# Attention: q loaded straight into the block-diagonal operand, instead of copied there by VectorE

## The reference, cut to what matters

```python
x = x + 0.5 * ffn(layernorm(x))          # weights and activations rounded to FP6 in blocks of 32
x = x + attention(layernorm(x))
x = x + 0.5 * ffn(layernorm(x))

# attention: 16 heads of 32, each token sees 13 neighbours (K = 13, NS = 6)
q, k, v = split(x @ qkv_w.T + qkv_b); q = q * 32 ** -0.5
ni = clip(i - NS, 0, L - K)              # first neighbour of token i
attn = softmax(einsum('bhld,bhlkd->bhlk', q, k[ni + j]) + rpb[:, bidx])
out = einsum('bhlk,bhlkd->bhld', attn, v[ni + j]) @ proj_w.T + proj_b
```

## Time and profile before

| | |
|---|---|
| runs | 3541.88, 3539.46, 3540.44 us |
| span of the profiled execution, first to last instruction | 3541.7 us |
| first phase with the setup | 0 to 1743 us |
| attention | 1743 to 3029 us |
| last phase | 3029 to 3541.7 us |
| busy share of the span: TensorE, VectorE, ScalarE, GpSimd | 82%, 78%, 57%, 56% |
| mean granted TensorE clock | 0.931 |

### The profile page before, as it was taken

One profiled execution on the slowest core, in us unless ns is written; L12 is line 12 of the kernel. 1 busy time (PEld: TensorE's weight loads), 2 busy tenths in 40 slices (PEclk: granted clock), 3 DMA queues, 4 the chain that ended last, 5 costly groups with the idle time before them and its releaser, 6 DMA issues. The chain is left out here.

```text
span 3541.7 us, 67789 instructions
## 1 busy us (share of the span) xinstructions
PE 2897.5 (82%) x24864; PEld 1690.4 (48%) x24864; DVE 2759.5 (78%) x3553; ACT 2021.9 (57%) x2451; POOL 1993.0 (56%) x1497
## 2 busy tenths in 40 slices
PE   0399999999999999999677777777777777399999
PEld 0244444444444444444356555555555555244444
DVE  7366666666666666666599999999999998599995
ACT  3355556555556555564566666666666657466553
POOL 3454455544555445543166665666666666588883
PEclk9699999999999999999889988999999889699999
DMA  2123332333323332332465554555555553234432
GB/s 72 60 84 119 108 108 95 108 111 115 102 101 107 107 119 93 103 114 84 146 175 163 170 170 148 166 161 179 152 162 162 169 160 98 107 143 155 153 142 83
DMA packets 274586, 449.41 MB, mean 127 GB/s; under 512 B 15368, under 2 KB 181280, under 8 KB 266144
## 3 DMA queue, kind: packets, MB, share of 16 engines
q1 hardware_dynamic: 274336, 445.54, 39.4%
HBM read 243.85 MB, written 201.38 MB: 126 GB/s over the span
## 5 line engine op out<-in xcount | busy, mean ns | idle before, releaser
L761 DVE TENSOR_TENSOR fq_out_lo<-fq_val,fq_out_hi 128x512 f16<-128x512 f32 x384 | 460.6, 1237 | 289.8 <-ACT fq_out_hi L825 289.8
L1125 DVE COPY att_q_bd<-att_q_in 32x1024 f16<-32x1024 f16 x512 | 624.0, 1219 | 5.9 <-DMA att_q_in<-q_parts 0.7
L942 PE MATMUL fq_acc<-fq_y_hi_t,w_qkv 128*128 128x512 f16 x2048 | 614.3, 379 | 1.6 <-ACT fq_y_hi_t L838 1.6
L825 ACT CAST fq_out_hi<-fq_val 128x512 f16<-128x512 f32 x384 | 237.2, 618 | 318.9 <-DVE fq_val L758 310.8
L1250 PE MATMUL att_s_ps<-att_k,att_q_bd 128*128 128x44 f16 x6144 | 192.0, 187 | 271.2 <-DVE att_q_bd L1125 251.0
L942 PE MATMUL fq_acc<-fq_y_lo_t,w_qkv 128*128 128x512 f16 x1024 | 388.1, 379 | 0.0
L1228 POOL TENSOR_TENSOR att_score<-att_score,att_rtotal 128x704 f32<-128x704 f32 x128 | 211.2, 1650 | 226.3 <-DVE att_rtotal L1116 226.3
L1210 POOL TENSOR_TENSOR att_score<-att_score,att_top 128x704 f32<-128x704 f32 x128 | 188.3, 1471 | 245.1 <-DVE att_top L1105 245.1
L1165 ACT ACTIVATE att_ctx<-att_o_ps 32x512 f32<-32x512 f32 x512 | 300.6, 587 | 44.8 <-PE att_o_ps L1275 38.6
L1285 PE MATMUL att_y_ps<-w_proj,att_ctx_t_hi 128*128 128x512 f16 x1024 | 320.3, 396 | 2.4 <-DVE att_x L1150 2.2
L1250 PEld LDWEIGHTS att_s_ps<-att_k,att_q_bd 128*128 128x128 f16 x6144 | 178.8, 100 | 290.9 <-issue 238.3
(11 more groups left out here) (189 smaller groups left out, 6707.1 us busy)
## 6 DMA issues: line engine op xcount, KB each, us to landing
att_v<-v_parts SPq DMA_DIRECT2D x96, 704.0 KB
att_k<-k_parts SPq DMA_DIRECT2D x64, 524.0 KB, 7.4
fq_x<-in_L_attn_x SPq DMA_DIRECT2D x32, 1024.0 KB, 6.9
x_after_ffn<-fq_x SPq DMA_DIRECT2D x32, 1024.0 KB, 4.3
att_q_in<-q_parts SPq DMA_DIRECT2D x32, 1024.0 KB, 7.2
att_x<-x_after_ffn SPq DMA_DIRECT2D x32, 1024.0 KB, 5.6
x_after_attention<-att_x SPq DMA_DIRECT2D x32, 1024.0 KB, 4.3
ffn_x_ring<-x_after_attention SPq DMA_DIRECT2D x32, 1024.0 KB, 6.2
```

Source lines behind the costliest of these rows:

```text
L761: dve.tensor_tensor(out=out[1][:, b], in0=val[:, b % RING], in1=out[0][:, b], op=ALU.subtract).then_inc(s["out_lo"], 1)
L825: act.copy(out[0][:, b], val[:, b % RING]).then_inc(s["out_hi"], 1)
L942: op = pe.matmul(acc[:, b % RING], w, m, start=(kc == 0 and (a, c) == (0, 0)), stop=(kc == KC - 1 and (a, c) == PARTS[-1]))
L1125: op = dve.tensor_copy(q_bd[rows, u.u % 2, :, :, :, h, :].rearrange("p a g c q -> p (a g) c q"), q_in[rows, g.u, :, :, place * P:(place + ...
```

## The change

In the first phase the blocks of q are moved out of PSUM in another order: inside 128 tokens, the query number q (0 to 31) is the outer index and the chunk c (0 to 3) the inner. So in HBM the four chunks' elements of one q stand together. In attention `q_in` and the copies are gone. `q_bd` is laid out as partition x half x unit of the half x part x kc x 128 columns x 4 chunks. A run of 32 q x 4 c, 256 bytes, goes straight from HBM to its head's block. For half a group (two units) that is 4 heads x 2 units x 2 parts = 16 DMAs of 32 partitions, each with 128 runs. The matmuls read the operand of a chunk at a step of 4 columns (8 bytes). SyncE's order is new. VectorE takes the second half of the transposed probabilities from ScalarE, and the orders of VectorE's and GpSimd's turns are changed.

```diff
@@ ffn_qkv_phase, hi_of_block
-                        act.activation(val[:, b % RING], acc[:, b % RING], ACT.Identity, bias=k.qk_bias[:, b:b + 1],
+                        value, total = val[:, b % RING], acc[:, b % RING]
+                        if b < KC:
+                            value = value.rearrange("p (a q c) -> p a q c", a=SUB, q=CHUNK)
+                            total = total.rearrange("p (a c q) -> p a q c", a=SUB, q=CHUNK)
+                        act.activation(value, total, ACT.Identity, bias=k.qk_bias[:, b:b + 1],
@@ attention_phase
+    QUNITS = UG // 2
-        q_in = sb("q_in", [P, 2, 2, KC, GROUP], F16)
-        q_bd = sb("q_bd", [P, 2, 2, KC, CHUNKS, HG, CHUNK], F16)
+        q_bd = sb("q_bd", [P, 2, QUNITS, 2, KC, P, CHUNKS], F16)
@@ sync
-                def queries_and_keys(g):
+                def queries(g, half):
                     if not g.within(GROUPS):
                         return
-                    need(sp, s["spread"], (g.n - 1) * UG)
-                    sp.dma_start(q_in[:, g.u].rearrange("p a g n -> p a (g n)"), ...)
+                    need(sp, s["scored"], (2 * g.n + half - 1) * QUNITS * PAIRS)
+                    if isinstance(g.h, int) and g.n == 0:
+                        sp.wait_ge(s["q_zero"], half + 1)
+                    for h in range(HG):
+                        rows = slice(h * HEAD_DIM, (h + 1) * HEAD_DIM)
+                        columns = scratch["q"][:, rows, bass.ds(g.n * KC * GROUP, KC * GROUP)].rearrange(
+                            "a p (g v n) -> v p a g n", g=KC, n=P)
+                        for unit in range(QUNITS):
+                            for part in range(2):
+                                sp.dma_start(q_bd[rows, half, unit, part, :, rows, :].rearrange("p g m c -> p g (m c)"),
+                                             columns[half * QUNITS + unit, :, part]).then_inc(q_loaded[half], 16)
...
+                def body(t):
+                    keys_in(t)
+                    values(t.back(1))
+                    queries(t, 0)
+                    residual_out(t.back(3))
+                    queries(t, 1)
+                    residual_in(t.back(1))
@@ vector
-                dve.memset(q_bd[:], 0.0).then_inc(s["q_zero"], 1)
-                dve.wait_ge(s["q_zero"], 1)
+                for i in range(2):
+                    dve.memset(q_bd[:, i], 0.0).then_inc(s["q_zero"], 1)
...
-                    for h in range(HG):
-                        rows = slice(h * HEAD_DIM, (h + 1) * HEAD_DIM)
-                        op = dve.tensor_copy(q_bd[rows, ...], q_in[rows, ...])
-                    op.then_inc(s["spread"], 1)
+                def second_half(u):
+                    need(dve, s["turned"], PAIRS * u.n + 2)
+                    need(dve, s["weighted"], u.n - 1)
+                    dve.tensor_copy(prob_t[:, u.u % 2, HALF:], t_ps[:]).then_inc(s["out_second"], 1)
...
# VectorE's turn: bias(t-1), totals(t-2), residual sum(t-7), second_half(t-4), low part of the context(t-6)
@@ scalar
-                    if w.within(UNITS):
-                        need(act, s["turned"], PAIRS * w.n + 2)
-                        act.copy(prob_t[:, w.u % 2, HALF:], t_ps[:]).then_inc(s["out_second"], 1)
@@ gpsimd
# its turn: low part of the probabilities(t-3), subtract the maximum(t-1), normalise(t-2), bias on x(t-6)
@@ tensor, scores
-                    need(pe, s["spread"], u.n + 1)
+                    half = place // QUNITS
+                    if place % QUNITS == 0:
+                        pe.wait_ge(q_loaded[half], 16 * HG * QUNITS * 2 * (g.n + 1))
...
-                                    q = q_bd[:, u.u % 2, a, kc, c].rearrange("p h q -> p (h q)")
+                                    q = q_bd[:, half, place % QUNITS, a, kc, :, c]
```

More of the change, by code:

```diff
@@ L1059, in queries_and_keys @@
                             k_loaded[g.u], 16)
-                def body(t):
[L1062 to L1078, removed]
@@ new lines, in values @@
+                def values(g):
+                    if not g.within(GROUPS):
+                        return
+                    need(sp, s["weighted"], (g.n - 1) * UG)
+                    sp.wait_ge(s["v_zero"], 2)
+                    for part, at in ((0, 0), (0, WIN), (1, 0)):
+                        rows = scratch["v"][part, bass.ds(g.n * GROUP, GROUP + 2 * NS), :]
+                        windows = bass.AP(rows.tensor, rows.offset, [[C, WIN], [CHUNK * C, GROUP // CHUNK], [1, C]])
+                        sp.dma_start(vals[at:at + WIN, g.u, :, part, :], windows).then_inc(v_loaded[g.u], 16)
@@ new lines, in residual_out, with residual_in @@
+                def residual_out(g):
+                    if not g.within(GROUPS):
+                        return
+                    need(sp, s["summed"], (g.n + 1) * UG)
+                    sp.dma_start(dst_v[:, bass.ds(g.n * UG, UG), :], x[:, g.u]).then_inc(stored[g.u], 16)
+                def residual_in(g):
+                    if not g.within(GROUPS):
+                        return
+                    need(sp, stored[g.u], 16 * g.h)
+                    sp.dma_start(x[:, g.u], src_v[:, bass.ds(g.n * UG, UG), :]).then_inc(x_loaded[g.u], 16)
@@ L1133, in body @@
                         bias(u)
-                    if t.within(UNITS):
-                        spread(t)
                     u = t.back(LAG_N)
@@ L1138, in body @@
                         totals(u)
[L1139 to L1144, removed]
                     u = t.back(LAG_OUT)
@@ L1152, in body @@
                                                  op1=ALU.add).then_inc(s["summed"], 1)
+                    u = t.back(LAG_T)
+                    if u.within(UNITS):
+                        second_half(u)
+                    u = t.back(LAG_C)
+                    if u.within(UNITS):
+                        need(dve, s["ctx_hi"], u.n + 1)
+                        need(dve, s["projected"], u.n - 1)
+                        dve.tensor_tensor(out=ctx_t[1][:, u.u % 2], in0=ctx_f[:, u.u % 2], in1=ctx_t[0][:, u.u % 2],
+                                          op=ALU.subtract).then_inc(s["ctx_lo"], 1)
                 run(dve, body)
@@ L1206, in body @@
                 def body(t):
+                    u = t.back(LAG_P)
+                    if u.within(UNITS):
+                        need(pool, s["p_hi"], u.n + 1)
+                        pool.tensor_tensor(out=prob[:, u.u % 2, :, WIN:2 * WIN], in0=score[:, u.u % 4],
+                                           in1=prob[:, u.u % 2, :, 0:WIN], op=ALU.subtract).then_inc(s["p_lo"], 1)
                     u = t.back(LAG_S)
@@ L1212, in body @@
                                            op=ALU.subtract).then_inc(s["lowered"], 1)
+                    u = t.back(LAG_N)
+                    if u.within(UNITS):
+                        need(pool, s["inverted"], u.n + 1)
+                        pool.tensor_tensor(out=score[:, u.u % 4], in0=score[:, u.u % 4],
+                                           in1=rtotal[:, u.u % 2].unsqueeze(2).to_broadcast(wide),
+                                           op=ALU.mult).then_inc(s["normed"], 1)
                     u = t.back(LAG_C)
```

27 lines of the change are left out of this document (4 added, 23 removed).

## The result

The changed kernel takes 3416.26 us (median of 4 runs, 3413.85 to 3418.23), the kernel before in the same runs 3539.95 us (3537.19 to 3541.88): ratio 0.9649, 95% interval 0.9636 to 0.9663. The gain is 124 us where 289 were forecast. The time lies inside the wide range (3200 to 3420), at its very end, and outside the forecast's own range (3225 to 3290). The profiled execution took 3418.23 us, with a span of 3416.3 us.

A forecast was written before the change was run, and what follows sets the result against it. VectorE was taken as the bound before, TensorE with transfers and SyncE's order after: 7.45 us a turn, 127 turns 946 us, bias adds to 2703.6, plus 37 and 512.3 us: span 3253, median 3252 us; range 3200 to 3420, own range 3225 to 3290.

The forecast's parts named there:

- VectorE bounds the kernel and stops doing so: Attention: VectorE, 94% busy, sets the turn; losing 4.96 us of copies and gaining 0.7, its turn falls to 5.2 us.
- TensorE's turn of 6.5 us: Attention: TensorE's work without waits, 3.00 + 3.04 + 0.45 us a turn, the longest of the four engines.
- The branch: Attention loop's branch: 4.23 us stall and about 1 us slower work, once in 8 turns, 0.65 us a turn.
- SyncE: the step that failed: SyncE's DMA issues: 39 a group instead of 8; q loads at 0.56 us each, 18 us a group.
- The room is there: SyncE has time for the new issues: two of its waits make 27 us of each 39.6 us group.
- How the parts meet: Compute 28.6 us and transfers 28.3 us a group, with up to 2.9 us of pause: 29.8 us a group.
- The rival with SyncE's issue as the bound: Loads held by full rings at 1.29 us each: a group takes 47 us, 3804 us in all; chance 0.06.
- the strided load: Rival: the scores' strided weight load costs 1.45 us, TensorE 8.6 us a turn, 3398 us; chance 0.07.
- the small packets: Rival: q's 256-byte packets cost as much as 1 KB ones, transfers 34.3 us a group, 3398 us; chance 0.10.
- The reordering at nothing: New step orders in attention cost nothing: the longest chain between turns is 4.4 us, under TensorE's 6.5.
- Transfers 28.3 us a group: DMA engines' transfers one after another: 12.8 us for v, 9.2 for other loads, 6.3 for q.
- pauses of the rings: Rings (packets issued, not yet moved) run empty through SyncE's queue order: up to 2.9 us a group.

The follow-up runs named there:

- after: The changed kernel itself, with 32 loads of q a group and v issued before the first half's q, against the kernel before: 3416.26 us, ratio 0.9649.
- The best kernel: The changed kernel with 8 loads of q a half, loop unrolled by 16 units, v issued behind the first half's q: 3218.17 us, ratio 0.9076.
- the kernel with 16 units: The kernel with 8 loads of q a half, its attention loop unrolled by 16 units instead of 8: 3253.45 us, ratio 0.9194.

## Why the prediction was right in kind and wrong in size

- **VectorE bounds the kernel and stops doing so: right.** The kernel without copies shows the price, 274 us. VectorE's share fell to 65% (about 70 forecast), and it waits for TensorE. `second_half` takes 0.68 us (0.7 forecast).
- **TensorE's turn of 6.5 us: nearly right.** It is 6.86 us undisturbed. The difference is the strided read, taken at nothing. The rival had its mechanism, at 1.45 us; it is 0.37. I had taken 0 because the rows show contiguous loads alone, and that was no reason to take the low end.
- **The branch: short.** The forecast took 4.23 us from one row. The six stalls of this kind in the trace of the kernel before are 4.2 to 5.8 us, 5.2 on average (31.4 / 6); in after they are 2.9 to 8.3, 5.5 on average (71.9 / 13). The slower work behind one is 2.4 us (5.93 - 3.49), and about 1 was forecast. So the 0.65 us a turn should have been (5.5 + 2.4) / 8 = 1.0. The slower work behind TensorE's other stops was not in the forecast.
- **SyncE: the step that failed.** The forecast gave 0.56 us to a load of q, 18 us to a group's 32, and said "The room is there". The unit price was nearly right: the half that isn't behind v takes 9.1 to 11.3 us in after, 0.57 to 0.71 a load, some 20 us for 32. The sum was not: the "How the parts meet" part let the other half's loads come "while v fills the rings" at no price to SyncE. In fact v's three loads and the half behind them take 22.2 us of the queue (20 to 24), where the sum had 9.0 for the half and the row 1.29 for a load of v, 12.9 at most. And the room was measured against the old group of 39.6 us: 18 us for q and 6 for the rest leave 15 of it, but only 6 of the forecast's own 29.8, less than the hold takes. The queue fills all 35 us of the new group. The rival with SyncE's issue as the bound was the right mechanism, at 35 us a group for its 47, with a chance of 0.06. It had all loads held alike; in the group shown the first behind v is held for 3.42 us and the other 15 take 0.63 each, (12.82 - 3.42) / 15. Halving the issues (154 us), swapping v and q (107 us) and shrinking v (179 us) each gain on it. That the measured time is still inside the wide range is luck: its upper end was set by two rivals, the strided load and the small packets, and neither of them is what set the time.
- **Small packets: right to be cheap.** Three quarters of them are worth 25 us, not the 146 of the rival. Twice as many of 128 bytes are not cheap.
- **The reordering at nothing: not contradicted.** Moving the half back changes 6 us, inside the intervals; the other orders were not put back.
- **Transfers 28.3 us a group: not contradicted.** The best kernel runs groups of 28.9 us at a DMA share of 0.87.

In terms of turns: with the issues halved a turn was 7.63 us, and with 4 loads and the contiguous read 7.31. That the forecast's 7.45 lies between is chance: I had no strided read and less branch, and pauses of the rings that didn't show.

Two rules of the Trainium skill bear on this. Its page "TensorE: Matmul & The Clock Gate", section "Weight-path perf modes — Fast Weight Load (FWL) and DoubleRow", gave a reason for a low chance of the strided rival, as it lets the fast load read packed or strided columns. It gives no price for a stride. The runs show none at step 2 (97 ns for 96) and one at step 4 (118 ns). "DMA: Bandwidth & Descriptors", section "Issuing engines are not separate DMA queues", calls a sequencer's time to initiate a DMA usually small beside the DMA. For one load that holds here, some 0.6 us against 3.0 from issue to landing; but 32 of them stand in one queue, and their 20 us are more than half of a group's 35.

What stays open: whether it is full rings that hold a load; how the hold and the order of landing combine when v stands between the heads; and why the branch stalls TensorE for 2.9 us at one time and for 8.3 at another in the same kernel. No run issued the loads of q and of v from two engines, which would part SyncE's queue from what the DMA engines can take.

## What to carry to other kernels

Price a queue by what stands in front of each issue, not by issues times their unhindered length: a load that is held holds every one behind it. When a copy on an engine is traded for DMAs, make few loads of many packets, and issue the large ones whose data is needed last behind the small ones needed first. When an engine's waits look like room, ask whether the new work can start where the waits are.

## What the runs showed that I had not expected

- One load of v held SyncE for 5.94 us and the load of q behind it for 3.42 us, while such loads take 0.3 to 0.4 us where nothing holds them.
- The load of the stationary operand takes 96 ns at step 1, 97 at step 2 and 118 at step 4 of float16; the matmuls follow at 25 and 33 ns.
- Packets of 256 bytes cost little (25 us for three quarters of them), and 8192 packets of 128 bytes a group some 114 us more than half as many of 256 (an estimate from two runs' difference, 78 us, and the 36 us of the read).
- The stall at TensorE's loop branch was 4.2 to 5.8 us before, 3.4 to 6.4 in the kernel with 16 units and 2.9 to 8.3 in after, and the work behind one of them took 2.4 us more, at a granted clock of 0.63.
